# Moving a layer's output stores from SyncE's queue to ScalarE's, with one input pair and some weight preparation moved to later groups

## The chip, the cores and the metric

The kernel runs on one core of a Trainium2 chip. The metric is the device time of one execution in microseconds, from launch to end. A profiled execution also has a span, from the first to the last instruction of the core, and a granted clock of TensorE.

## The reference, cut to what matters

The input x has the shape (4, 16, 512, 512). Four residual layers follow each other, each with a group normalisation in front of a convolution. The change touches the first layer only, and in it the first of its two blocks:

```
x = x + L0(gn(x))            # 8 groups of 2 channels for each image
L0: y = block1(gn(x)); z = block2(y)
block(v): for every channel, its triplet of neighbouring channels is convolved with three
          reflected 5x5 kernels of dilation 1, 2 and 4, weighted by a, b, c, summed, then tanh
x = x + L1(gn(x))            # 3x3 convolution of quantised values
x = x + L2(gn(x))            # 17x17 box filter
x = x + L3(gn(x))            # convolution in the frequency domain
```

## The kernel before, in words

Function `layer0` holds the whole first layer. The work of a block is cut into units u: an image b, a pair of channels p (8 pairs for each image) and a half of the rows, so NU = 64 units for a block and 16 for an image. A unit has four groups g, and n = 4u + g counts groups: n = 0 to 255 is the first block, 256 to 511 the second. For a first-block group TensorE runs 27 offsets times 4 matmuls (L726) from a window tile `win[half]`, which holds the rows of neighbouring channels as two fp16 halves. ScalarE takes the result out of PSUM through tanh (`evict`, L804), VectorE splits it into a high and a low fp16 part in the tile `yt[u % 2]` (`halves`, L631 and L633), GpSimd mirrors the margins (L896), and the group's rows are stored to the DRAM tensor `ys` (`store_y`, L957). A group makes two such stores; it makes three where p is 0 or 7, that is in the first two and the last two units of an image, because the edge channels are written twice.

The windows are loaded two units ahead from the DRAM tensor `xs` (`load`, L939): two transfers for a group, four where p is 0. A load for unit u waits for the matmuls that read the same place of the window in unit u - 2. In the units with u % 16 == 2, and in unit 0, the four loads are put together behind the third group (`late`).

`xs` is made in the same stretch. For a pair i of input channels (32 in all, 8 for each image) there are four steps z = 0 to 3 in four consecutive groups, starting at `first_group(i)`: statistics on VectorE (`v0`, L457), their sums over partitions by two small matmuls (`p0`, L703 and `p1_`, L707), the root on ScalarE (`root_step`, L240, with an activation table load before and after it), the scaling and the split (`v2` L473, `hi` L795, `v3` L479), the margins (L851), and the store of the pair (`store_xs`, L912). Pairs 0 and 1 come before the first group, pair 2 has steps around groups 0 and 1, pair 3 starts at group 4, pair 4 at group 11, and then one every 7 groups. The input of pair i (`load_x`, L905) is loaded 4 and 6 groups after the start of pair i - 2.

The order on each engine is written out by hand. SyncE's queue issues, for each group n in turn: the store of a finished pair, the window loads of two units later, the stores of `ys` for group n (each waits for the margins of group n, semaphore `c_pad`), and the next quarter of input. ScalarE's order for a group is: root, evict, `hi`. An eviction of group n waits for VectorE's `halves` of group n - 3, and a group's matmuls wait for the eviction of group n - 4, because there are four PSUM banks and three tiles `c_t`. `halves` of the first group of a unit waits until all `ys` stores of unit u - 2 have landed (`c_yd`).

`channel_weights` (L548 to L577) and `scaled_weights` on VectorE make weights for later layers. The first follows a matmul (L783) behind group 8 and ends in a sum for which TensorE waits with a matmul (L786) behind group 11. The second comes in group 15, with a root on ScalarE.

Of the kernel before, what the change touches and what calls it, by code (L numbers as in the profile page):

```python
# [16 lines left out]
RW = 2 * PW  # L17
CP = 32 * RW
VP = 2 * CP
# [264 lines left out]
def layer0(K):  # L284
# [6 lines left out]
    NU = NB * 16  # L291
    NG = 8 * NB

    with ExitStack() as ctx:
# [62 lines left out]
        def place(u):  # L357
            blk, r = divmod(u, NU)
            b, q = divmod(r, 16)
            return blk, b, q // 2, q % 2  # L360

        def first_group(i):

            image, j = divmod(i - 3, 8)
            return 64 * image + 4 + 7 * j if i > 2 else -2

        steps = {first_group(i) + z: (i, z) for i in range(2, NG) for z in range(4) if first_group(i) + z >= 0}
        loads_x = {first_group(i - 2) + 4 + 2 * c: (i, c) for i in range(4, NG) for c in range(2)}
# [81 lines left out]
        with nc.Block() as block:  # L450

            @block.vector
            def _(v):
# [223 lines left out]
                for u in range(2 * NU):  # L677
                    blk, b, p, half = place(u)
                    for g in range(4):
                        if doubled(4 * u + g + 1):  # L680
                            copies(4 * u + g + 1)
                        i, s = stage_of(4 * u + g)
                        if i is not None:
                            (v0, v1, v2, v3)[s](i)
                        if (u, g) == (2, 0):
                            mark["v"] = ch.n
                        if (u, g) == (2, 1):
                            channel_weights()
                        if (u, g) == (3, 3):
                            scaled_weights()  # L690
                        if table_of(u) is not None and g % 2 == 0:
                            table(table_of(u), g // 2)
                        (total if blk else halves)(u, g)
                        if blk:
                            extremes(u, g)
                    if blk:
                        gather(u)

            @block.tensor
            def _(p):  # L700
                def p0(i):
                    p.wait_ge(a_v, mark["m", i])
                    p.matmul(ap[:, 0:1], ones[:, :], am[:, :, 0], start=True, stop=True).then_inc(a_p, 1)  # L703

                def p1_(i):
                    p.wait_ge(a_v, mark["d", i])
                    p.matmul(ap[:, 1:2], ones[:, :], d0, start=True, stop=True).then_inc(a_p, 1)  # L707

                def products(u, g):
                    blk, b, pr, half = place(u)  # L710
                    n = 4 * u + g
                    pg, buf, wu = pp[:, n % 4, :], win[half], wc2[pr % 2] if blk else wc[pr % 2][:, 0]
                    rows_in(p, u, g)
                    if (u, g) == (2, 0):
                        p.wait_ge(w_sw, 32)
                    if (u, g) == (NU, 0):
                        p.wait_ge(w_s2, 16 * 24)
                        p.wait_ge(w_wn, 12)
                    if n >= 4:
                        p.wait_ge(c_act, n - 3)  # L720

                    def four(weights, source, at, start=False, stop=False):
                        for j in range(4):
                            bk = 4 * g + j
                            var = 0 if (half, bk) == (0, 0) else (2 if (half, bk) == (1, 15) else 1)
                            t = p.matmul(pg[32 * j:32 * j + 32, :], weights[:, var], source[:, j, at:at + NW],  # L726
                                         start=start, stop=stop, tile_position=(0, 32 * j))
                        return t

                    rows4 = buf[:, 4 * g:4 * g + 4]  # L730
                    for di in (4, 0, 1, 7, 8):
                        for wl, xl in ((0, 0), (0, 1), (1, 0)):
                            four(wu[:, wl, :, di], rows4, xl * PW + PAD + DX[di], start=(di, wl, xl) == (4, 0, 0))
                    i, s = stage_of(n - 1)
                    if s == 0:
                        p0(i)
                    if s == 1:
                        p1_(i)
                    for di in (2, 3, 5, 6):
                        t = four(wu[:, 1, :, di], rows4, PAD + DX[di])  # L740
                    if not blk:
                        for di in (2, 3, 5, 6):
                            for xl in range(2):
                                t = four(wu[:, 0, :, di], rows4, xl * PW + PAD + DX[di], stop=(di, xl) == (6, 1))
                    if blk:
                        p.wait_ge(c_nh, n_copied(n))
                        p.wait_ge(c_nl, n_copied(n))
                        for e, di in enumerate((2, 3, 5, 6)):
                            four(wn2[pr % 2][:, :, e], near[n % 2], PAD + DX[di])
                        p.wait_ge(c_2a, n_copied(n))  # L750
                        p.wait_ge(c_2b, n_copied(n))
                        four(wn2[pr % 2][:, :, 4], twice[n % 2], PAD - 2)
                        t = four(wn2[pr % 2][:, :, 5], twice[n % 2], PAD - 1, stop=True)
                    t.then_inc(c_pe, 1)

                p0(0)
                p1_(0)
                p0(1)
                p1_(1)
                p.wait_ge(w_ld, 320)  # L760
                p.wait_ge(a_v, mark["we"])
                for d in range(3):
                    t = p.matmul(p1[0:96, 0:18], emb[:, d, :], we[:, :, d, :], start=d == 0, stop=d == 2)
                t.then_inc(w_p, 1)
                p.wait_ge(a_v, mark["sum"])
                p.matmul(p1[:, 32:34], ones[0:27, :], c2[0:27, 0:2], start=True, stop=True).then_inc(w_p, 1)
                p.wait_ge(w_sel, 16)
                p.wait_ge(a_v, mark["cch"])
                for var in range(3):
                    for col in range(32):  # L770
                        t = p.matmul(p3[:, var, col // 16, 18 * (col % 16):18 * (col % 16) + 18], sel[:, var, col, :],
                                     cch[:, :], start=True, stop=True)
                t.then_inc(w_p, 1)
                p0(2)
                p1_(2)
                p.wait_ge(a_v, mark["wc"])
                for u in range(2 * NU):
                    for g in range(4):
                        products(u, g)
                        if (u, g) == (2, 0):  # L780
                            p.wait_ge(w13_ld, 160)
                            p.wait_ge(a_v, mark["v"])
                            p.matmul(pq[:, 0:432], rep[:, :], w16[:, :, :].rearrange("p j n -> p (j n)"), start=True, stop=True).then_inc(w13_p, 1)  # L783
                        if (u, g) == (2, 3):
                            p.wait_ge(a_v, mark["g3"])
                            p.matmul(pq[:, 0:1], ones[:, :], c2b[:, 0:1], start=True, stop=True).then_inc(w13_p, 1)  # L786

            @block.scalar
            def _(s):
# [17 lines left out]
                def copies(n):  # L807
                    w = four_rows(s, n)
                    s.activation(twice[n % 2][64:128, :, PAD - 2:PAD - 1 + NW], w[0:64, :, PW + PAD + 1:PW + PAD + 2 + NW], ACT.Copy).then_inc(c_2b, 1)  # L809
                    s.activation(twice[n % 2][0:64, :, PAD - 2:PAD - 1 + NW], w[0:64, :, PW + PAD - 2:PW + PAD - 1 + NW], ACT.Copy).then_inc(c_2a, 1)  # L810

                for blk in range(2):
                    pre = f"L0_conv_blk{blk + 1}_"
                    for d, nm in enumerate("abc"):
# [16 lines left out]
                for u in range(2 * NU):  # L831
                    for g in range(4):
# [2 lines left out]
                            copies(4 * u + g + 1)  # L835
                        if st_ == 2:
                            root_step(s, a_v, mark["rt", i], a_rt, ve, sq)
                        if (u, g) == (3, 3):
                            root_step(s, a_v, mark["sv"], w13_rt, c2b[:, 1:2], c2b[:, 2:3])
                        evict(u, g)  # L840
                        if st_ == 2:
                            hi(i)

            @block.gpsimd
            def _(q):
# [53 lines left out]
            def _(e):  # L899
# [49 lines left out]
                    for m in range(2):  # L949
                        e.dma_start(xwin(u)[m::2], rows(x, u, m, NW, NH * NW)).then_inc(c_xd[u % 2], 16)  # L950

                def store_y(u, g):
                    blk, b, p, half = place(u)
                    e.wait_ge(c_pad, 8 * u + 2 * g + 2)
                    y = yt[u % 2][:, g].rearrange("p l w -> p (l w)")
                    for m, gp, slot in [(0, p, 1), (1, p + 1, 0)] + [(1, 0, 0)] * (p == 0) + [(0, 8, 1)] * (p == 7):
                        e.dma_start(dram(ys, pair(b, gp, slot, 16 * half) + g * 4 * RW, [[RW, 4], [VP, 16], [1, RW]]), y[m::2]).then_inc(c_yd[u % 2], 16)  # L957

                def store_x1(u, g):
                    e.wait_ge(c_lo, 4 * u + g + 1)  # L960
                    blk, b, p, half = place(u)
# [32 lines left out]
                for u in range(2 * NU):  # L994
                    blk, b, p, half = place(u)
                    late = u < NU and u % 16 == 2 or u == 0
                    for g in range(4):
# [14 lines left out]
                                load(u + 2, gg)  # L1012
                        if blk:
                            store_x1(u, g)
                        else:
                            store_y(u, g)
                        if g == 0 and NU + 2 <= u + 1 < 2 * NU:
                            load_res(u + 1)
                        if g == 0 and u in (NU - 4, NU - 3):
# [1056 lines left out]
```

## Time and profile before

| | |
|---|---|
| median of 3 runs | 5208.22 us (5204.88 to 5220.45) |
| profiled execution, its own time | 5213.77 us |
| its span | 5212.0 us |
| mean granted TensorE clock | 0.986 |
| TensorE matmul busy | 4885.1 us, 94% of the span |
| first block's groups, first matmul to last | 71.4 to 1669.8 us |

Times within the trace are microseconds from the start of the span. The busy share of TensorE is high, so what can be won or lost lies in the places where it waits, and in the half clock that follows some of these waits.

### The profile page before, as it was taken

Reading aid. Unit: us, or ns where it says so; the run is one execution under the profiler, and the core shown is the slowest. Engines: PE = TensorE matmul, PEld = TensorE weight load, DVE = VectorE, ACT = ScalarE, POOL = GpSimd, SP = SyncE. Lnnn points to the kernel's source line nnn. Section 1 sums busy time; section 2 is a strip of 40 time slices with the busy share of each in tenths; the row PEclk is TensorE's granted clock in tenths of the full one; section 3 lists DMA queues with packets and bytes.
Section 4 is the critical chain, followed back from the end, with each engine's and each line's share of the span. In section 5 each row is a group of like instructions: output and inputs, shape, how many; then the busy total and the mean of one; then the engine's idle time right before and its main releaser. Section 6 shows DMA issues by size and latency. Waiting matters only on the chain. (4 is left out here: it accounts for less than half of the span.)

```text
span 5212.0 us, 176617 instructions
## 1 busy us (share of the span) xinstructions
PE 4885.1 (94%) x76605; PEld 2764.2 (53%) x76605; DVE 3722.4 (71%) x6707; ACT 3385.1 (65%) x3511; POOL 1419.1 (27%) x1641
## 2 busy tenths in 40 slices
PE   4999999999999999999999979997777899999998
PEld 2444444444445566555456653444555566666665
DVE  5653453453433888888888868887999688888888
ACT  2231222222222788888888878885998689899897
POOL 0000001000001222222222200002777255555556
PEclk9999999999999999999999989999999999999999
DMA  8777777677666788778787869996887465655664
GB/s 248 240 256 232 232 251 240 229 254 240 221 225 182 233 221 228 234 222 243 231 233 238 221 210 325 323 323 243 309 308 269 115 152 149 153 149 153 153 149 120
DMA packets 355854, 1167.09 MB, mean 224 GB/s; under 512 B 58409, under 2 KB 59048, under 8 KB 285226
## 3 DMA queue, kind: packets, MB, share of 16 engines
q1 hardware_dynamic: 352920, 1153.41, 72.0%
q8 instruction: 606, 9.93, 0.8%
q10 hardware_dynamic: 2162, 2.39, 0.2%
q14 instruction: 166, 1.36, 0.1%
HBM read 683.58 MB, written 453.51 MB: 218 GB/s over the span
## 5 line engine op out<-in xcount | busy, mean ns | idle before, releaser
L726 PE MATMUL c_p<-c_w,wc 128*32 128x512 f16 x27648 | 1527.6, 382 | 25.3 <-DMA c_w<-xs 22.5
L804 ACT ACTIVATE c_t<-c_p,cbias,cscale 128x512 f32<-128x512 f32 x512 | 398.1, 778 | 1292.0 <-PE c_p L726 1292.0
L726 PEld LDWEIGHTS c_p<-c_w,wc 128*32 128x32 f16 x27648 | 737.6, 97 | 786.7 <-issue 34.7
L726 PE MATMUL c_p<-c_w,w 128*32 128x512 f16 x19456 | 1131.6, 379 | 7.0 <-issue 5.6
L726 PEld LDWEIGHTS c_p<-c_w,w 128*32 128x32 f16 x19456 | 641.7, 96 | 431.7 <-issue 12.8
L631 DVE TENSOR_SCALAR c_y<-c_t 128x512 f16<-128x512 f32 x256 | 109.6, 428 | 702.7 <-ACT c_t L804 576.6
L1801 PE MATMUL f_P<-f_qh,f_wt 64*64 64x512 f16 x4608 | 545.7, 378 | 1.8 <-DVE f_t L1697 1.8
L1801 PE MATMUL f_P<-f_hl,f_wt 64*64 64x512 f16 x4608 | 545.3, 379 | 0.0
L809 ACT ACTIVATE c<-c_w 64x2052 f16<-64x2052 f16 x256 | 492.5, 1924 | 12.3 <-DMA c_w<-ys 6.0
L810 ACT ACTIVATE c<-c_w 64x2052 f16<-64x2052 f16 x256 | 493.0, 1926 | 6.3
L1962 POOL TENSOR_TENSOR f_y<-f_y,f_x 128x512 f32<-128x512 f32 x256 | 331.1, 1293 | 448.1 <-DVE f_hl L1676 442.0
L896 POOL COPY c_y<-c_y 128x16 f16<-128x16 f16 x512 | 88.5, 203 | 1269.0 <-DVE c_y L633 1269.0
L1697 DVE SCALAR_TENSOR_TENSOR f_t<-f_P,f_kk,f_ci 128x256 f32<-128x256 f32 x1024 | 423.5, 476 | 11.9 <-PE f_P L1801 7.2
L1561 POOL TENSOR_TENSOR e_hl<-e_g,e_hl 128x2048 f16<-128x2048 f32 x63 | 257.3, 4083 | 608.0 <-ACT e_hl L1511 608.0
L1762 PE MATMUL f_qp<-f_hil,f_gT 128*128 128x260 f16 (+1 forms) x3120 | 393.4, 276 | 4.0 <-DVE f_qh L1681 4.0
L1801 PEld LDWEIGHTS f_P<-f_hl,f_wt 64*64 64x64 f16 x4608 | 232.9, 106 | 255.0 <-issue 77.7
L1190 PE MATMUL d_pp<-d_q,wq 128*128 128x512 f16 x1536 | 345.9, 381 | 16.9 <-DVE d_q L1087 16.9
L1968 POOL TENSOR_TENSOR f_t<-f_t 128x512 f32<-128x512 f32 (+1 forms) x260 | 334.1, 1285 | 71.8 <-DVE f_hl L1676 71.8
L1936 ACT ACTIVATE f_y<-f_P,f_kk,sv 128x256 f32<-128x256 f32 x512 | 261.3, 561 | 127.5 <-PE f_P L1801 121.2
L641 DVE TENSOR_TENSOR a_x<-c_t,a_x 128x512 f32<-128x512 f32 x256 | 192.7, 753 | 199.9 <-ACT c_t L804 174.5
L1762 PEld LDWEIGHTS f_qp<-f_hil,f_gT 128*128 128x128 f16 (+1 forms) x3120 | 295.2, 98 | 42.2 <-issue 4.9
L1681 DVE SCALAR_TENSOR_TENSOR f_qh<-f_qp,f_qh 128x520 f16<-128x520 f32 (+1 forms) x260 | 181.9, 700 | 179.9 <-ACT f_qh L1915 179.8
(274 smaller groups left out, 7789.2 us busy)
## 6 DMA issues: line engine op xcount, KB each, us to landing
c_w<-xs SPq DMA_DIRECT2D x576, 264.0 KB, 7.6
d_x<-x SPq DMA_DIRECT2D x128, 1024.0 KB, 7.7
x<-d_x SPq DMA_DIRECT2D x128, 1024.0 KB, 5.1
ys<-c_y SPq DMA_DIRECT2D x576, 132.0 KB
c_w<-ys SPq DMA_DIRECT2D x144, 528.0 KB
xs<-a_hl SPq DMA_DIRECT2D x70, 1056.0 KB, 11.4
a_x<-in_x SPq DMA_DIRECT2D x256, 256.0 KB, 5.7
a_x<-in_x SPq DMA_DIRECT2D x128, 512.0 KB, 4.9
```

Source lines behind the costliest of these rows:

```text
L726: t = p.matmul(pg[32 * j:32 * j + 32, :], weights[:, var], source[:, j, at:at + NW], start=start, stop=stop, tile_position=(0, 32 * j))
L804: s.activation(tt_[n % 3][:, :], pp[:, n % 4, :], ACT.Tanh, bias=cbias[:, blk:blk + 1], scale=cscale[:, blk:blk + 1]).then_inc(c_act, 1)
L809: s.activation(twice[n % 2][64:128, :, PAD - 2:PAD - 1 + NW], w[0:64, :, PW + PAD + 1:PW + PAD + 2 + NW], ACT.Copy).then_inc(c_2b, 1)
L810: s.activation(twice[n % 2][0:64, :, PAD - 2:PAD - 1 + NW], w[0:64, :, PW + PAD - 2:PW + PAD - 1 + NW], ACT.Copy).then_inc(c_2a, 1)
L1190: t = p.matmul(pp[:, 4 * (i % 2) + j, :], wq[:, wl, dx, :], qt[i % NQ][:, j, dx:dx + NW], start=(i < 2 and dx == 0 and wl == 0), stop=(i > ...
L1561: q.tensor_tensor(h[:, 1], gt[i % 2][:, :, :], h[:, 0], ALU.subtract).then_inc(e_lo, 1)
L1697: v.scalar_tensor_tensor(dst[0:n, z], src[:, 256 * z:256 * z + 256], k_[0:n, off + z:off + z + 1], cc_[0:n, j, z], op, ALU.mult).then_inc( ...
L1762: t = p.matmul(qp[0:n, a_, 0:260], T[:, xl, 1 - a_, kx, 0:n], hil[:, wl, 1 - a_, kx, :], start=z == 0, stop=z == 5)
L1801: t = p.matmul(P[64 * z:64 * z + 64, bank, :].rearrange("p (a i) -> p a i", a=2), w[k0:k0 + 64, wl, f, :], r[k0:k0 + 64, l, :, 0:256], sta ...
L1936: s.activation(y0[i % 3][0:n, z], P[0:n, 0, 256 * z:256 * z + 256], ACT.Identity, bias=k_[0:n, 6 + z:7 + z], scale=inv(i)).then_inc(f_y0, 1)
L1962: q.tensor_tensor(y0[i % 3][:, :, :], y0[i % 3][:, :, :], par(xin[i % NXF][:, :]), ALU.add).then_inc(f_ax, 1)
L1968: q.tensor_tensor(t1[i % 3][0:n], t1[i % 3][0:n], t2[i % 2][0:n], ALU.add).then_inc(f_aw, 1)
```

## The change

The stores of `ys` leave SyncE's queue. ScalarE issues those of group n - 1 in its turn of group n, behind the eviction of n and behind `hi` if there is one, so the first block's last group is stored in the first turn of the second block. Pair 3 starts at group 6 in place of 4, and the input of pair 5 is therefore loaded at groups 10 and 12 in place of 8 and 10. The first weight matmul moves from behind group 8 to behind group 14, `channel_weights` from group 9 to 15, the second weight matmul from behind 11 to behind 17, and `scaled_weights` from group 15 to 22. No instruction is added or left out.

```
-            return 64 * image + 4 + 7 * j if i > 2 else -2
+            return 64 * image + 4 + 7 * j + 2 * (i == 3) if i > 2 else -2
...
-                        if (u, g) == (2, 0):
+                        if (u, g) == (3, 2):
                             mark["v"] = ch.n
-                        if (u, g) == (2, 1):
+                        if (u, g) == (3, 3):
                             channel_weights()
-                        if (u, g) == (3, 3):
+                        if (u, g) == (5, 2):
                             scaled_weights()
...
-                        if (u, g) == (2, 0):
+                        if (u, g) == (3, 2):
                             p.wait_ge(w13_ld, 160)
...
-                        if (u, g) == (2, 3):
+                        if (u, g) == (4, 1):
                             p.wait_ge(a_v, mark["g3"])
...
+                def store_y(u, g):
+                    blk, b, p, half = place(u)
+                    s.wait_ge(c_pad, 8 * u + 2 * g + 2)
+                    y = yt[u % 2][:, g].rearrange("p l w -> p (l w)")
+                    for m, gp, slot in [(0, p, 1), (1, p + 1, 0)] + [(1, 0, 0)] * (p == 0) + [(0, 8, 1)] * (p == 7):
+                        s.dma_start(dram(ys, pair(b, gp, slot, 16 * half) + g * 4 * RW, [[RW, 4], [VP, 16], [1, RW]]), y[m::2]).then_inc(c_yd[u % 2], 16)
...
-                        if (u, g) == (3, 3):
+                        if (u, g) == (5, 2):
                             root_step(s, a_v, mark["sv"], w13_rt, c2b[:, 1:2], c2b[:, 2:3])
                         evict(u, g)
                         if st_ == 2:
                             hi(i)
+                        if 1 <= 4 * u + g <= 4 * NU:
+                            store_y(*divmod(4 * u + g - 1, 4))
...
                         if blk:
                             store_x1(u, g)
-                        else:
-                            store_y(u, g)
```

## Rows read from the trace of the kernel before

**Rows 1.** Waits of TensorE, then of SyncE's queue, over the first block's groups.

```profile
PE a_p L707 <- DVE f_t L465: 22.7, 3, 9.6
PE c_p L726 <- DMA c_w<-xs: 22.5, 7, 5.9
PE a_p L703 <- DVE a_mv L459: 6.1, 2, 4.1
PE a_p L786 <- DVE c2b L577: 3.9, 1, 3.9
...
SPq L957 <- POOL c_y L896: 44.9, 46, 5.3
```

**Rows 2.** ScalarE's timeline: evictions of groups 68, 80, 132, 144, 196, 208.

```profile
502.25 0.78 ACT L804 ACTIVATE c_t<-c_p,cbias,cscale 128x512 f32<-128x512 f32 x1 [5.06 <-PE c_p L726]
...
596.23 0.78 ACT L804 ACTIVATE c_t<-c_p,cbias,cscale 128x512 f32<-128x512 f32 x1 [13.64 <-PE c_p L726]
...
907.46 0.78 ACT L804 ACTIVATE c_t<-c_p,cbias,cscale 128x512 f32<-128x512 f32 x1 [5.06 <-PE c_p L726]
...
995.63 0.78 ACT L804 ACTIVATE c_t<-c_p,cbias,cscale 128x512 f32<-128x512 f32 x1 [13.14 <-PE c_p L726]
...
1304.93 0.78 ACT L804 ACTIVATE c_t<-c_p,cbias,cscale 128x512 f32<-128x512 f32 x1 [5.06 <-PE c_p L726]
...
1392.53 0.78 ACT L804 ACTIVATE c_t<-c_p,cbias,cscale 128x512 f32<-128x512 f32 x1 [11.47 <-PE c_p L726]
```

**Rows 3.** TensorE's timeline at the first image boundary.

```profile
522.87 0.59 PE L707 MATMUL a_p<-f_t,ones 128*128 128x1 f32 x2 [9.59 <-DVE f_t L465]
...
587.62 12.66 PE L726 MATMUL c_p<-c_w,wc 128*32 128x512 f16 x184 [5.86 <-DMA c_w<-xs]
```

**Rows 4.** VectorE's timeline there, and its waits over the block.

```profile
521.13 0.43 DVE L631 TENSOR_SCALAR c_y<-c_t 128x512 f16<-128x512 f32 x1 [17.60 <-DMA ys<-c_y]
...
DVE c_y L631 <- DMA ys<-c_y: 124.2, 13, 17.6
```

**Rows 5.** SyncE queue's timeline there: issues, with start and length.

```profile
506.40 2.60 SPq L957 DMA_DIRECT2D ys<-c_y  x3
...
533.74 3.44 SPq L957 DMA_DIRECT2D ys<-c_y  x3
537.28 1.76 SPq L939 DMA_DIRECT2D c_w<-xs  x2
539.09 3.29 SPq L957 DMA_DIRECT2D ys<-c_y  x3
```

**Rows 6.** DMA view of 510 to 550 us: 40 slices of 1 us.

```profile
DMA  4883223973222893226952269532398222298322
GB/s 133 264 302 129 101 97 123 294 247 150 101 87 99 272 344 115 101 95 188 342 194 96 95 177 308 222 126 87 127 291 275 106 112 111 95 285 315 141 88 101
```

**Rows 7.** DMA view of 71 to 1670 us: issues.

```profile
c_w<-xs SPq DMA_DIRECT2D x566, 264.0 KB, 8.1
ys<-c_y SPq DMA_DIRECT2D x567, 132.0 KB
xs<-a_hl SPq DMA_DIRECT2D x67, 1056.0 KB, 11.5
a_x<-in_x SPq DMA_DIRECT2D x232, 256.0 KB, 5.6
```

**Rows 8.** Timeline at the start: TensorE's waits, ScalarE's eviction of group 5.

```profile
111.70 0.59 PE L703 MATMUL a_p<-a_mv,ones 128*128 128x1 f32 x2 [4.07 <-DVE a_mv L459]
...
130.59 6.02 PE L726 MATMUL c_p<-c_w,wc 128*32 128x512 f16 x108 [2.18 <-DMA c_w<-xs]
...
116.37 0.78 ACT L804 ACTIVATE c_t<-c_p,cbias,cscale 128x512 f32<-128x512 f32 x1 [11.16 <-PE c_p L726]
```

**Rows 9.** SyncE queue's stores: in a quiet stretch (600 to 841), and at the start.

```profile
L957 SPq DMA_DIRECT2D ys<-c_y x84: 542/568/2338, 600.0 to 841.0; - x84
...
100.81 13.53 SPq L957 DMA_DIRECT2D ys<-c_y  x6
```

More of the change, by code:

```diff
@@ L950, in load_res @@
                         e.dma_start(xwin(u)[m::2], rows(x, u, m, NW, NH * NW)).then_inc(c_xd[u % 2], 16)
[L952 to L957, printed above, removed]
                 def store_x1(u, g):
```

## The prediction

> **What bounds the kernel now.** I read the waits first. Over the first block's groups TensorE waits for four things: the statistics matmuls for VectorE (22.7 and 6.1 us), the window loads (22.5 us), and once for the weight sum (3.9 us) [rows 1]. That is 55 us in which nothing else stands in its way; the rest of the block's 1598 us is matmuls. So this change can win only in these places and in the half clock behind them, and it can lose wherever it makes a new one.
>
> Then I read where the waits lie. A quiet group takes 5.84 us: 0.78 of eviction and 5.06 of idle time on ScalarE [rows 2]. Two evictions twelve groups apart should be 70.0 us apart, and up to 2.4 more where four of the groups carry statistics matmuls (0.59 us each [rows 3]). At the three image boundaries it is 93.98, 88.17 and 87.60 us [rows 2]. The excess is 21.6, 15.8 and 15.2 us, together 52.6.
>
> Third, who makes it. In the first of them TensorE waits 9.59 us in a statistics matmul and 5.86 us for a window [rows 3]; the other 6 us are slower matmuls behind these waits and small gaps. VectorE is late for the statistics because it stands for 17.60 us in front of tile `c_y`, until the stores of the unit before the last have landed; over the block it stands so for 124.2 us [rows 4]. The last of those stores was issued at 506.40 to 509.00 and the tile came free at 521.13 [rows 4, 5]. So a store lands about 12 us after SyncE is rid of it: it isn't issue alone that is late, there is a queue of work behind it.
>
> Fourth, what the queue waits for. SyncE is solid here: 3.44 us for three stores, 1.76 for two loads, 5.35 us from one group's stores to the next (533.74 to 539.09) [rows 5]. One reads this easily as an issuing engine at its limit. But a store takes 0.568 us to issue in a quiet stretch [rows 9], and here 1.1. The slices say why: between short bursts of 264 to 344 GB/s the DMA engines are busy for two to three tenths, at 87 to 127 GB/s [rows 6]. The stores run on about a quarter of the 16 engines, and that quarter is full. The bursts are the loads, which use all.
>
> From this I price the full quarter: a store moves 132 KB at about 100 GB/s, 1.35 us. Three of them leave (5.35 - 4.05) / 2 = 0.65 us for a load of 264 KB, so 2.6 us for a store of `xs` (1056 KB) and 0.63 for 256 KB of input. Over the block that makes 567 x 1.35 + 566 x 0.65 + 67 x 2.6 + 232 x 0.63 = 765 + 368 + 174 + 146 = 1453 us [rows 7], 91% of 1598. In a quiet group it is 2 x 1.35 + 2 x 0.65 + (8 x 0.63 + 2 x 2.6) / 7 = 5.5 us of 5.84. In the eight groups before an image boundary (three stores, four loads) it is 4.05 + 2.6 + 1.5 = 8.15, in the eight behind it 6.85. The overload is 8 x 2.3 + 8 x 1.0 = 26 us; buffers take some of it, and 15 to 22 are left as the excess seen.
>
> **The change part by part.**
>
> *The stores' queue.* SyncE loses 567 issues and their `c_pad` waits (44.9 us [rows 1]); its loads go out as soon as the window is free. ScalarE gets these issues. In quiet groups two cost 2 x 0.57 = 1.1 us of 5.06 idle: nothing, covered by that idle time. In the turn with root and `hi` there is less room, but an eviction may be three groups late (17.5 us) before TensorE waits for its bank, so again nothing; without that cover it would be 1.1 us in 30 turns, 33 us. The wait on `c_pad` is for the group before, 5.84 us old, so it is met. Where VectorE is held up it isn't, and behind it stand the next eviction, then VectorE's next `halves`, then the matmuls four groups on.
>
> The 52.6 us are another matter. The quarter has the same 26 us too much at each boundary, whoever issues. Only what the buffers can take differs. Before, loads and stores were one line, so both were late together. Now they are two lines. The loads have eight groups of lead and need it less; the stores stand alone in theirs, and their lateness becomes ScalarE's, because a full ring holds the issuing engine (that is what 1.1 us for an issue of 0.57 shows). Each side of it has a bound. Below: the loads give way, the stores land in time and all 52.6 us go. Above: the trace shows three stores at 13.53 / 2 = 6.8 us at the start, where all engines are full [rows 9]. With 0.78 of eviction that is 7.6 us a group, 1.7 over 5.84, in 48 boundary groups 82 us. I take +5 us for each boundary, +15: nearest to the row of the full quarter, 3.44 + 0.78 = 4.2 us [rows 5], which fits in 5.84 but leaves little when a root and `hi` come in the same turn.
>
> The Trainium skill (DMA: Bandwidth & Descriptors, "Issuing engines are not separate DMA queues") says that issuing from several engines saves only the issuing time, as all share the same 16 engines. By it the boundaries keep their 52.6 us, a term of 0 here in place of my +15.
>
> *Pair 3 two groups later.* TensorE waits 4.07 us in group 5 for the statistics of pair 3, and eviction 5 comes 0.78 + 11.16 = 11.94 us after eviction 4, 6.1 too many [rows 8]. Two groups are 11.7 us, more than the 4.07 that its input was late: -6. The 2.18 us for the window of group 8 [rows 8] should go as well, since the loads of unit 2 no longer queue behind six stores that took 13.53 us [rows 9]: -2. Against that the pair's store comes two groups later, and the loads of unit 4 wait for it; they are issued at group 11 for group 16, 29 us of lead against 11.5 of landing for the store and 8.1 for a load [rows 7]: nothing, and 10 us if it fails. Stores of both queues fill the start, where the engines are full anyway: +2. Sum -6, from -8 to +4.
>
> *The weights.* The same 50-odd instructions and two matmuls in the same distance (6 groups later, between statistics steps in the same way): TensorE's 3.9 us wait for the sum [rows 1] goes along. ScalarE's turn 16 now holds a store that waits for VectorE to finish them. Before, VectorE began them in the turn of group 9 and TensorE waited 3.9 us for their end behind group 11, so they end some 3 x 5.84 + 3.9 = 21 us after their group begins; the eviction of group 17 is due at 17.5 and comes 4 us late or a little more, within 17.5. Term 0, from -2 to +4.
>
> *The end of the block.* ScalarE stores groups 254 and 255 in turns that also hold the second block's copies: -0, +5, taken as 0.
>
> Sum: +15 - 6 + 0 = +9 us on 5213.77 (span 5212.0 and 1.8 around it), which is 5.5 above the median: 5208.22 + 9, about **5217 us**.
>
> **The rivals.** (1) *The boundary waits go.* If what is full is SyncE's line and not the quarter of the engines, the stores are issued right behind the next eviction (four groups before that of 502.25 [rows 2], so at about 480 in place of 506), VectorE's 17.6 us vanish, and TensorE loses none: -52.6 - 8 = -61, 5147 us; with half the effect 5178. For it: SyncE has no gap there [rows 5]. Against: 1.1 us for an issue that needs 0.57, and slices at two tenths [rows 6]. The Trainium skill (Perfetto Trace Analysis, "DMA Optimizations") recommends it: if descriptor generation is the bottleneck, spread the DMAs over issuing engines, and loads and stores over two. That would be this case. Chance 0.27.
>
> (2) *ScalarE is held by its stores.* Slower: if an issue at the boundaries takes over (5.84 - 0.78) / 3 = 1.69 us, ScalarE falls behind for good, evictions come late, and TensorE waits for banks. At 2.25 us it is +82; with the start's gain and some groups below that, +20 to +80, say 5250 us. It also decides if loads and stores share the engines piece by piece, since a load's pieces are larger. For it: the start's row [rows 9]. Against: the full quarter itself needs only 1.35 us for a store. Chance 0.25.
>
> (3) *It does nothing.* The wait keeps its size and only its name changes, 5208 - 6 = 5202 us. Chance 0.10.
>
> **How the numbers follow.** The forecast has 0.38; its own range is 5195 to 5240. 0.3% is 15.6 us, about what a measurement of this kernel can tell. Below 5192.6 lies most of rival 1 and a little of the forecast: 0.29. Above 5223.8 lies rival 2 and a quarter of the forecast: 0.34. The rest, 0.37, is within. The range leaves out the far parts of rivals 1 and 2: 5160 to 5265.
>
> **What would show it.** Right: in 440 to 600 us the DMA slices keep their stretches of two to three tenths; VectorE waits less for `ys` but for ScalarE instead; issues on ScalarE take about 1.1 us at the boundaries; evictions twelve groups apart there still are 88 to 100 us apart; groups 4 and 5 are 5.8 to 6.3 apart. Wrong: boundaries at 72 us (rival 1), or evictions late in quiet stretches too, with TensorE waiting for ScalarE (rival 2). The forecast fails if the engines serve the two queues unevenly: then either the loads or the stores take the whole overload, and eight groups of lead or three groups of banks decide it.

## The result, and the profile after

The changed kernel takes 5251.76 us (median of 4 runs, 5241.35 to 5257.96), the kernel before 5207.48 in the same comparison: a ratio of 1.0075, 95% interval 1.0061 to 1.009. It is slower by 0.75%, 32 to 47 us by the interval and 44 by the medians, where 5217 was forecast; 5251.76 lies in the range, on the side of the second rival (ScalarE is held by its stores, 5250). The profiled span is 5248.3 us against 5212.0, 36.3 more, and the mean granted clock 0.983 against 0.986.

Where the time went is read from one kind of row, the evictions on ScalarE's timeline (L804), taken at the same group in both traces. Groups are counted by the evictions themselves, 512 in each trace; two that follow each other without a gap stand in one merged row of a timeline. The column on the right is how late the changed kernel is.

| eviction of group | before, us | after, us | after is late by |
|---|---|---|---|
| 4 | 104.43 | 103.43 | -1.0 |
| 22 | 229.26 | 238.51 | 9.3 |
| 50 | 396.18 | 405.80 | 9.6 |
| 80 (first boundary passed) | 596.23 | 605.41 | 9.2 |
| 144 (second) | 995.63 | 1006.53 | 10.9 |
| 208 (third) | 1392.53 | 1406.32 | 13.8 |
| 250 | 1640.62 | 1654.15 | 13.5 |
| 256 | 1675.63 | 1716.61 | 41.0 |
| 270 | 1757.19 | 1789.90 | 32.7 |

So the start (groups 4 to 22) costs 10.3 us, the stretches with the three boundaries 4 us together, and the end of the block 27.5, of which 8.3 come back in the second block's first groups. Of the 36.3 us between the spans, 32.7 are there at group 270.

The waits of the changed kernel, from 71 to 1740 us, which takes in the first block and the second's first groups: engine, tile and line, what it waited for, then the sum in us, times, the longest.

```profile
ACT c_t L804 <- PE c_p L726: 906.4, 214, 14.5
DVE c_y L631 <- ACT c_t L804: 729.2, 162, 31.4
ACT c_t L804 <- issue: 224.0, 28, 31.8
...
PE a_p L703 <- DVE a_mv L459: 43.0, 5, 11.8
PE c_p L726 <- DVE c_n L662: 20.9, 1, 20.9
...
PE c_p L726 <- ACT c_t L804: 14.9, 4, 6.5
...
PE a_p L786 <- DVE c2b L577: 5.7, 1, 5.7
PE c_p L726 <- DMA c_w<-xs: 3.7, 1, 3.7
```

TensorE's waits add up to 88 us where they were 55 in the block [rows 1], or 59 up to 1740 us. The window loads are no longer late (3.7 us for 22.5), and VectorE waits no more for stores of `ys` (124.2 us [rows 4]): it waits for ScalarE. ScalarE in turn has 224 us of idle time ahead of evictions that nothing released but its own issuing. A reader who looks at TensorE's releasers alone would blame VectorE (64 us); VectorE waits for an eviction, and the eviction for an issue.

ScalarE's timeline shows what it issues: at the start, before the first image boundary, and at the end of the block.

```profile
103.43 9.71 ACTq L817 DMA_DIRECT2D ys<-c_y  x3
113.25 0.78 ACT L804 ACTIVATE c_t<-c_p,cbias,cscale 128x512 f32<-128x512 f32 x1 [9.04 <-issue]
113.27 10.43 ACTq L817 DMA_DIRECT2D ys<-c_y  x3
...
453.36 10.43 ACTq L817 DMA_DIRECT2D ys<-c_y  x3
...
469.63 15.49 ACTq L817 DMA_DIRECT2D ys<-c_y  x3
485.23 0.78 ACT L804 ACTIVATE c_t<-c_p,cbias,cscale 128x512 f32<-128x512 f32 x1 [14.85 <-issue]
485.26 14.56 ACTq L817 DMA_DIRECT2D ys<-c_y  x3
...
1667.38 32.46 ACTq L817 DMA_DIRECT2D ys<-c_y  x3
1699.95 0.78 ACT L804 ACTIVATE c_t<-c_p,cbias,cscale 128x512 f32<-128x512 f32 x1 [31.80 <-issue]
```

Three stores hold ScalarE for 10, 15 and once 32 us, where the group leaves 5.06. Behind the last of them stand the eviction at 1699.95, 28 us after its matmuls were done, VectorE's work on it, and TensorE, which waits 20.9 us for its next input `c_n` until 1708.29. The grouped issues of line 817 give the usual figure beside it (shortest, median and longest in ns; 200 to 440 us, then 445 to 545 us):

```profile
L817 ACTq DMA_DIRECT2D ys<-c_y x80: 515/527/5599, 206.7 to 438.0; - x80
...
L817 ACTq DMA_DIRECT2D ys<-c_y x39: 515/1282/9437, 447.5 to 539.9; - x39
```

The queue of SyncE, in the same two places:

```profile
472.13 8.58 SPq L948 DMA_DIRECT2D c_w<-xs  x12
...
482.87 28.30 SPq L948 DMA_DIRECT2D c_w<-xs  x10
...
1659.98 16.65 SPq L944 DMA_DIRECT2D c_w<-ys  x16
...
1683.32 5.77 SPq L944 DMA_DIRECT2D c_w<-ys  x8
1718.12 1.14 SPq L965 DMA_DIRECT2D x<-a_x  x2
```

Its loads go in bursts now; [rows 5] has two loads between two lots of stores. From 1689.09 to 1718.12 it issues nothing, and ScalarE is held until 1699.84 all the same. So it isn't an issue of SyncE that ScalarE waits for there.

The DMA view of 510 to 550 us, as in [rows 6]. There are now twelve slices in a row at 91 to 99 GB/s, at two tenths:

```profile
DMA  2794223972327853222222222222329842228932
GB/s 97 215 376 150 112 96 126 294 275 108 137 87 190 289 218 123 93 91 99 95 97 97 97 97 97 95 99 95 116 95 272 243 190 114 84 101 240 361 138 115
```

### The profile page after: what moved, and what is told of

It reads as the page before. It is cut to its first block and busy times, and to the rows that moved or that the text cites. A ratio compares the mean times of both kernels' runs of the same rounds, so it can differ in the third digit from the quotient of the medians.

```text
span 5248.3 us, 176617 instructions
## 1 busy us (share of the span) xinstructions
PE 4885.4 (93%) x76605; PEld 2851.3 (54%) x76605; DVE 3721.2 (71%) x6707; ACT 3384.2 (64%) x3511; POOL 1413.9 (27%) x1641
## 5 line engine op out<-in xcount | busy, mean ns | idle before, releaser
L804 ACT ACTIVATE c_t<-c_p,cbias,cscale 128x512 f32<-128x512 f32 x512 | 397.8, 777 | 1351.9 <-PE c_p L726 1107.2
L726 PEld LDWEIGHTS c_p<-c_w,w 128*32 128x32 f16 x19456 | 700.2, 96 | 368.7 <-issue 11.4
L726 PE MATMUL c_p<-c_n,w 128*32 128x512 f16 x4096 | 298.2, 380 | 23.0 <-DVE c_n L662 22.1
## 6 DMA issues: line engine op xcount, KB each, us to landing
xs<-a_hl SPq DMA_DIRECT2D x70, 1056.0 KB, 10.8
```

Of the source, the lines that this page charges most:

```text
L804: s.activation(tt_[n % 3][:, :], pp[:, n % 4, :], ACT.Tanh, bias=cbias[:, blk:blk + 1], scale=cscale[:, blk:blk + 1]).then_inc(c_act, 1)
```

## The experiments

The expectations name theories by letters. A is the second rival's mechanism: the stores run on a quarter of the engines, that quarter is full, and the engine that issues them is held. The others are rivals to it: SyncE's issuing is the limit (D), the two queues share something that makes the descriptors (E), loads and stores share an engine piece by piece, so that the size of a load's pieces decides (F), or only the engines' total time counts and not who is served first (G). Lines below are those of the changed kernel where nothing else is said. Each ratio is to the kernel before in the same comparison.

**1. The stores alone.** The changed kernel with pair 3 and both weight steps at their old places.

```
-            return 64 * image + 4 + 7 * j + 2 * (i == 3) if i > 2 else -2
+            return 64 * image + 4 + 7 * j if i > 2 else -2
...
-                        if (u, g) == (3, 2):
+                        if (u, g) == (2, 0):
...
```

> Only the stores' queue moves to ScalarE; pair 3 and the weights stay where they were. Theory A (the stores on ScalarE's queue carry the whole loss, because a load burst of SyncE holds the engines that the stores need): 5245 to 5265 us, +40 to +57 over before, with issues of three stores of 10 to 32 us on ScalarE at the start, at the image boundaries and at the end of the block. Rival B (the moved steps carry part of the loss): under 5235 us.

5252.59 us (5244.29 to 5256.62), ratio 1.0074 (1.005 to 1.0097). The whole loss is the stores'. The wait for the weight sum is 16.2 us here and 5.7 in the changed kernel, so the later weights seem to ease what the stores do at the start, though not in a total that can be measured. The rival that expected under 5235 us is out.

**2. The steps alone.** The kernel before with pair 3 and the weights moved, and the stores left with SyncE.

```
-            return 64 * image + 4 + 7 * j if i > 2 else -2
+            return 64 * image + 4 + 7 * j + 2 * (i == 3) if i > 2 else -2
...
-                        if (u, g) == (2, 0):
+                        if (u, g) == (3, 2):
...
```

> Only pair 3 and the weights move; the stores stay on SyncE's queue in their old form. After the run with the stores alone gave the whole loss, theory A: these steps are worth -2 to -8 us, as the 4.07 us wait in group 5 and the 2.18 us wait for the window of group 8 go and the wait for the weight sum moves along. Rival B: they cost 5 us or more, through the later store of pair 3 or a collision of the weights with the next pair.

5213.73 us (5208.26 to 5222.69, 12 runs), ratio 1.0012 (1.0004 to 1.0021): no gain. TensorE's timeline at the start says why:

```profile
127.64 5.97 PE L726 MATMUL c_p<-c_w,wc 128*32 128x512 f16 x60 [6.46 <-DMA c_w<-xs]
...
197.66 0.59 PE L786 MATMUL a_p<-c2b,ones 128*128 128x1 f32 x2 [5.42 <-DVE c2b L577]
```

The wait of 4.07 us in group 5 is gone, and the window of group 8 is 6.46 us late in place of 2.18 [rows 8]. The wait was returned one step further on. (The changed kernel doesn't have this wait: with the stores off SyncE's queue, TensorE ends group 11 at 147.61 us where it was 155.14.)

**3. The loads held back.** SyncE waits for the margins of each group in the place where it used to store, and issues nothing there.

```
+                        else:
+                            e.wait_ge(c_pad, 8 * u + 2 * g + 2)
```

> The changed kernel, but SyncE waits for the margins of group n where its stores of group n were, without storing. Theory A with the burst as its cause (SyncE, rid of these waits, sends the second block's first loads in one burst of 16): the stall of 32 us in the last groups of the block goes down to under 10, total 5215 to 5230 us. Theory C (any load in flight is enough, the order of issue does not matter): within 5 us of the changed kernel, 5247 to 5257 us.

5243.73 us (5237.82 to 5249.33), ratio 1.0055 (1.0035 to 1.0075). By the medians the bursts account for about 8 us, which the intervals don't settle, and the 5215 to 5230 expected was missed. At the end of the block three stores still take 21.70 us, where under 10 was expected. So bursts lengthen one stall; they aren't alone what makes the stores slow.

**4. The stores on all engines, issued by SyncE.** In the kernel before, the two plain stores of a group become four, one for each row. On the DRAM side their outer dimension is the 16 row blocks (`[VP, 16]`) and not the 4 rows (`[RW, 4]`).

```
-                    for m, gp, slot in [(0, p, 1), (1, p + 1, 0)] + [(1, 0, 0)] * (p == 0) + [(0, 8, 1)] * (p == 7):
-                        e.dma_start(dram(ys, pair(b, gp, slot, 16 * half) + g * 4 * RW, [[RW, 4], [VP, 16], [1, RW]]), y[m::2]).then_inc(c_yd[u % 2], 16)
+                    for j in range(4):
+                        e.dma_start(dram(ys, pair(b, p, 1, 16 * half) + (g * 4 + j) * RW, [[VP, 16], [31 * CP, 2], [1, RW]]),
+                                     y[32 * j:32 * j + 32]).then_inc(c_yd[u % 2], 16)
+                    for m, gp, slot in [(1, 0, 0)] * (p == 0) + [(0, 8, 1)] * (p == 7):
+                        ...
```

> The kernel before, with the two plain stores of a group written as four, each of 32 partitions with the 16 row blocks outermost on the DRAM side; the extra edge store stays. Same bytes and pieces. Theory A (a store in the old form runs on a quarter of the 16 engines, that quarter is full): the stores spread over all engines, the slices of two to three tenths vanish, boundaries fall from 88 to 94 us to 72 to 78 for twelve groups, total 5140 to 5165 us. Rival D (SyncE's issuing is the limit): 2 more issues of 0.57 us a group on a queue that is solid at the boundaries, total 5215 to 5240 us.

5235.53 us (5220.06 to 5241.72), ratio 1.0036 (1.002 to 1.0053): slower, where theory A expected 5140 to 5165. D had it right. SyncE's queue at the first boundary, and the DMA slices of 510 to 550 us:

```profile
507.18 2.49 SPq L957 DMA_DIRECT2D ys<-c_y  x4
509.71 0.57 SPq L960 DMA_DIRECT2D ys<-c_y  x1
510.39 2.65 SPq L939 DMA_DIRECT2D c_w<-xs  x4
513.08 2.51 SPq L957 DMA_DIRECT2D ys<-c_y  x4
```

```profile
DMA  9989975689697318999868863797469754378952
```

The stretches of two tenths are gone, most slices are at six to nine, so the work of the quarter is now spread. But the queue is still solid, now with each issue at its shortest, 0.6 us. Nine of them and their gaps take 5.9 us (507.18 to 513.08), and a group has 5.84. Here "solid" means what it seemed to mean in [rows 5], and there did not.

**5. The same stores issued by ScalarE.** The changed kernel with the four stores of experiment 4 in place of its two.

> The changed kernel with the stores spread in the same way, issued by ScalarE. Theory A (ScalarE is held by pieces in full engines): with 2 pieces for each engine and store nothing holds it, 5130 to 5165 us. Rival E (ScalarE's issue waits until SyncE's issue is through, as if one generator served both): twice the issues, twice the waits: 5250 to 5300 us.

5193.03 us (5186.34 to 5206.06), ratio 0.9965 (0.9952 to 0.9978), 59 us under the changed kernel though it issues almost twice as many stores. The row of ScalarE's queue from 71 to 1740 us (packets, MB, share of 16 engines), first of the changed kernel, then of this one:

```profile
q10 hardware_dynamic: 39168, 77.87, 12.7%
```

```profile
q10 hardware_dynamic: 53504, 77.92, 15.4%
```

39168 is 576 x 68: 64 pieces and 4 more for each store. 53504 is 1024 x 48 + 64 x 68: 32 pieces and 16 more for each new store. If the additional packets are one completion for each engine that a store uses, the old form uses 4 and the new one 16. The Trainium skill (DMA: Bandwidth & Descriptors, "Why a DMA increments its semaphore by 16 and not by 1") says just this: the number of engines is the largest one up to 16 that divides the slowest dimension of both sides, and each posts one completion. The old store has a slowest dimension of 4 on its DRAM side and of 64 on the other; the packets agree.

At the boundary the stores' issues now have a median of 617 ns where it was 1282:

```profile
L817 ACTq DMA_DIRECT2D ys<-c_y x69: 537/617/4092, 443.0 to 544.5; - x69
```

This speaks against E: almost twice the stores, and no issue above 4.1 us in this row. The expected 5130 to 5165 was missed all the same. What is left is, it seems, ScalarE's own time. Four or five issues of 0.6 us leave 2.1 to 2.7 of 5.06 us, which a turn with root and `hi` exceeds, and ScalarE's own issues stand ahead of 58 evictions with 374.7 us of idle time, 6.5 us each. Experiment 7 tries this.

**6. Only the third store spread.** In the changed kernel, the third store that the first and last pair of an image have is cut in four, each with 16 as the outer dimension; the plain stores stay.

```
+                    for m, gp, slot in [(1, 0, 0)] * (p == 0) + [(0, 8, 1)] * (p == 7):
+                        for j in range(4):
+                            s.dma_start(dram(ys, pair(b, gp, slot, 16 * half) + (g * 4 + j) * RW, [[VP, 16], [1, RW]]),
+                                        y[32 * j + m:32 * j + 32:2]).then_inc(c_yd[u % 2], 16)
```

> The changed kernel, with only the third store of edge groups written as four of 16 partitions; the two plain stores keep their old form. Theory A (a quarter of the engines is full at the image boundaries because of the third store): the boundary's load on that quarter falls from 8.15 and 6.85 us a group to about 7.1 and 5.8, the long issues of 10 to 15 us become fewer, and the total is 5210 to 5235 us. Rival D (the number of issues on ScalarE counts): six issues in place of three at the boundaries, 5255 to 5280 us.

5227.29 us (5221.08 to 5231.77), ratio 1.003 (1.0019 to 1.004). Taking a third of the load off the quarter in these groups, with more to issue, is worth 24 us. It bears out A: less load on the quarter, less loss.

**7. Spread, and the issuing shared.** SyncE issues rows 0 and 1 in its old place, ScalarE rows 2 and 3 and the third store.

```
+                    for j in (2, 3):
+                        s.dma_start(dram(ys, pair(b, p, 1, 16 * half) + (g * 4 + j) * RW, [[VP, 16], [31 * CP, 2], [1, RW]]),
+                                     y[32 * j:32 * j + 32]).then_inc(c_yd[u % 2], 16)
...
+                    e.wait_ge(c_pad, 8 * u + 2 * g + 2)
+                    y = yt[u % 2][:, g].rearrange("p l w -> p (l w)")
+                    for j in (0, 1):
+                        e.dma_start(...)
```

> The spread stores of the fifth run, but rows 0 and 1 of a group are issued by SyncE in the old place and rows 2 and 3 and the edge store by ScalarE. If what is left at 5193 us is ScalarE's time (5 issues of 0.62 us, beside root and hi) and in the fourth run SyncE's (6 to 9 issues a group), sharing helps both: 5150 to 5180 us. If SyncE's wait for the margins in front of its loads is what costs, it is 5190 to 5210 us.

5164.99 us (5164.37 to 5172.88), ratio 0.9918 (0.9904 to 0.9931). It beats both kernels, and experiment 5 by 28 us, so the time of issuing did count there.

**8. Small pieces, by another address pattern.** The loads of the first block with a dimension of its own for the rows.

```
-                                        dram(src, at + h8 * (8 * VP - RW), [[CP, 16], [RW, 2], [1, 4 * RW]])).then_inc(c_ld[half][g], 16)
+                                        dram(src, at + h8 * (8 * VP - RW), [[CP, 16], [RW, 2], [RW, 4], [1, RW]])).then_inc(c_ld[half][g], 16)
```

> The changed kernel, with the first block's window loads written as rows of 2112 bytes in place of runs of 8448 (same bytes, four times the pieces). Theory F (an engine that has work from both queues takes one piece from each in turn, so four times larger load pieces starve the stores): the pieces are now equal, three stores at a boundary take 4 to 7 us in place of 10 to 15 on ScalarE, and the total falls to 5215 to 5235 us. Rival G (the engines' time is what is short, whoever is served first): no change or slower, 5245 to 5270 us. If the run of four rows is joined again on its way to the engines, nothing changes and the trace still shows pieces of 8448 bytes.

5250.2 us (5243.58 to 5259.16), ratio 1.0079 (1.0063 to 1.0095). It says nothing: the trace has no more packets than before, so adjacent rows were joined again and the edit changed no piece.

**9. Half pieces in the first block.** Each of its loads becomes two, of two rows each, with pieces of 4224 bytes in place of 8448; the stores are as in the changed kernel.

```
+                            for r in (0, 2):
+                                e.dma_start(win[half][gp % 2 + 2 * h8:128:4, 4 * g + r:4 * g + r + 2].rearrange("p k w -> p (k w)"),
+                                            dram(src, at + h8 * (8 * VP - RW) + r * RW, [[CP, 16], [RW, 2], [1, 2 * RW]])).then_inc(c_ld[half][g], 16)
```

> The changed kernel, with every window load of the first block cut into two transfers of two rows, so that its pieces are 4224 bytes in place of 8448 (the earlier try was joined to 8448 again). Same bytes; SyncE issues 4 or 8 loads a group in place of 2 or 4. Theory F (an engine takes one piece of each queue in turn): at the boundaries 48 store pieces took 14.6 to 15.5 us, about 0.3 us each, as if each waited for one load piece of 0.2 to 0.4 us; with pieces half as large the longest issues of three stores there are 8 to 11 us and the total is 5222 to 5242 us. Rival G (only the engines' total time counts): the longest stay at 13 to 16 us, total 5247 to 5265 us.

5242.56 us (5239.74 to 5245.22), ratio 1.0049 (1.0034 to 1.0064) to 5218.74. ScalarE's timeline before the first boundary, the turns of groups 60 and 61:

```profile
469.37 10.31 ACTq L817 DMA_DIRECT2D ys<-c_y  x3
...
479.81 7.85 ACTq L817 DMA_DIRECT2D ys<-c_y  x3
```

15.49 and 14.56 us have become 10.31 and 7.85, as F has it. But later turns take longer in return: the stores of turns 58 to 68 take 78.1 us together, where they took 80.4. The total moves by less than the two comparisons can settle.

**10. Half pieces at the end of the block.** Only the second block's loads are cut in two: pieces of 8448 bytes in place of 16896.

```
+                                for r in (0, 4):
+                                    e.dma_start(win[half][first + gp % 2:first + 2 * count:2, 4 * g + r:4 * g + r + 4].rearrange("p k w -> p (k w)"),
+                                                dram(src, at + off + r * RW, [[CP, count], [1, 4 * RW]])).then_inc(c_ld[half][g], 16)
```

> The changed kernel, with the second block's window loads (whose first ones stand beside the last stores of the first block) cut in two, pieces of 8448 bytes in place of 16896. Theory F: the issue of three stores that took 32.5 us at the end of the block takes 16 to 22, and the total falls by 8 to 15 us, to 5237 to 5244 us. Rival G: it stays at 29 to 34 us and the total within 4 us of the changed kernel.

5249.91 us (5245.66 to 5253.85), ratio 1.0063 (1.0048 to 1.0078). ScalarE's timeline in place of the one issue of 32.46 us:

```profile
1665.73 11.20 ACTq L817 DMA_DIRECT2D ys<-c_y  x3
...
1677.06 14.16 ACTq L817 DMA_DIRECT2D ys<-c_y  x3
...
1691.35 12.01 ACTq L817 DMA_DIRECT2D ys<-c_y  x3
```

The longest hold is less than half as long, in the direction of F. But the same three turns sum to 37.4 us where it was 40.6 (32.46, 3.68 and 4.41), so next to nothing is won, and the 5237 to 5244 of F was missed. It looks as if the hold ends when the loads in front of the quarter are through, not after a number of stores. Nor is the piece the only thing that changed: SyncE now issues twice as many loads, and 32 of them take 25.58 us where 16 took 16.65, so the loads come more slowly too.

**11. The version of experiment 7 with the old steps.** Pair 3 and the weights back at their places.

> The shared, spread stores of the seventh run, with pair 3 and the weights where they were before the change. The run with the moved steps alone was 0.12% slower than before, since the wait in group 5 came back as a wait for the window of unit 2. If the steps are no help with spread stores either: 5155 to 5165 us. If they are, because the loads now come in time: 5168 to 5178 us.

5160.54 us (5157.48 to 5165.2), ratio 0.9895 (0.9878 to 0.9911). The interval overlaps that of experiment 7, so moving the steps later brings nothing here either. ScalarE before the first boundary:

```profile
484.46 0.78 ACT L804 ACTIVATE c_t<-c_p,cbias,cscale 128x512 f32<-128x512 f32 x1 [5.06 <-PE c_p L726]
484.46 1.19 ACTq L817 DMA_DIRECT2D ys<-c_y  x2
485.68 0.56 ACTq L820 DMA_DIRECT2D ys<-c_y  x1
490.29 0.78 ACT L804 ACTIVATE c_t<-c_p,cbias,cscale 128x512 f32<-128x512 f32 x1 [5.06 <-PE c_p L726]
```

Each issue takes its shortest time, each eviction waits 5.06 us for TensorE as in a quiet group, and the groups are 5.83 us apart. TensorE's waits in the block's groups are 3.4 us for windows, 5.5 and 2.8 for VectorE, and 11.8 in small gaps of issue.

## Why the prediction was right or wrong

**What bounds the kernel: right.** The reading that a quarter of the engines is full, and not SyncE, holds: the packets (experiment 5), the gain from taking load off it (5, 6, 7), and the slices that fill up (4). One part was too strong. Once the stores are spread, SyncE's issuing is the next limit, and a close one (4). The first rival, that the boundary waits simply go, came out wrong for the reason given: 1.1 us for an issue of 0.57, and slices at two tenths.

**The stores' queue at the boundaries: +15 forecast, 4 measured.** The direction and the mechanism were right, the size too high. The lateness did move from VectorE's wait for stores to ScalarE's issues, as "their lateness becomes ScalarE's" says, and it came earlier: ScalarE is late from turn 58 on, and TensorE loses time in groups 66 and 69, where it did in 70 and 80. The length of an issue, named as about 1.1 us, has a median of 1.28 but is very uneven; three of them took up to 15.49.

**The start: -6 forecast, +10.3 measured.** The first half of the forecast, -8 for pair 3 and the window, came about in the changed kernel: the last matmul of group 11 ends 7.5 us earlier than before, 1.0 of it because a weight matmul now comes later. (With the stores left on SyncE it doesn't, by experiment 2.) The step that failed is "Stores of both queues fill the start, where the engines are full anyway: +2". That the engines are full is no cover when the engine that is held is the one that evicts. ScalarE's turns 4 to 6 hold it for 9.71, 10.43 and 11.98 us, its eviction of group 9 comes 14.75 us after its matmuls, VectorE's statistics of pair 4 stand behind these evictions, and TensorE waits for them in group 12. Group 12 ends 20.90 us after group 11; before it was 14.44, with the wait for the weight sum in it.

```profile
162.69 0.58 PE L703 MATMUL a_p<-a_mv,ones 128*128 128x1 f32 x2 [11.84 <-DVE a_mv L459]
...
205.02 0.59 PE L786 MATMUL a_p<-c2b,ones 128*128 128x1 f32 x2 [5.68 <-DVE c2b L577]
```

So the held stores cost some 15 us at the start (20.90 in place of a quiet 5.84), where +2 was forecast. The row for it was in hand: six stores in 13.53 us [rows 9], which was used as an upper bound for the boundaries and not applied to the start itself, where it was read.

**The end of the block: 0 forecast, with +5 as its bound; +27.5 measured, 8.3 of them given back.** This is the largest miss, and the bound was wrong as well. The step is "ScalarE stores groups 254 and 255 in turns that also hold the second block's copies: -0, +5". It looked at ScalarE's work and not at what SyncE does there. SyncE, no longer held to a group's pace by its waits for `c_pad`, sent 16 of the second block's loads in one go at 1659.98 (before, eight went out between two lots of stores, 5.56 us at 1666.02), and the three stores of 1667.38 took 32.46 us among them. The forecast counted the waits that SyncE loses (44.9 us [rows 1]) as nothing but a gain for the loads.

**The weights: 0 forecast, about 0 measured.** What their sum cost in group 12, 14.44 us for 5.84, it costs in group 18 now, 14.27. The wait is 5.68 us for 3.93, and the eviction of group 17 comes 8.6 us late, not 4. The totals of experiments 1, 2 and 11 agree.

The terms measured, 10.3 + 4 + 19.2, come to 33.5 where +9 was forecast. So what took place is the second rival, and 5251.76 lies in the range because the range took it in. That its price, 5250, was so near is luck: it was priced by up to 82 us in 48 groups at the boundaries, which gave 4, and the loss came at the start and at the end of the block. Its second condition, "if loads and stores share the engines piece by piece, since a load's pieces are larger", is what experiments 9 and 10 agree with for the length of one hold. For the total they bear out little: 9 and 2 us by the medians. The sums of several turns hardly moved, so the total seems to follow the work that the quarter has before it.

**What stays open.** How an engine chooses between the two queues is seen only through these lengths. How much of the loss at the start is due to the loads that SyncE issues in it (sixteen for the windows from 116.36 us on), no run tells; with half the piece the evictions of groups 6 and 7 were 20.63 us apart, where it was 12.11 (experiment 9). The number of engines of a store and the piece size of the loads were not varied against each other, so the pieces' own share in the slow stores is open. At the end of the block there is one more candidate: two of every four loads of the second block have an outer dimension of 8 (L944). If they use 8 engines, as a store with 4 uses 4, and the stores' engines are among them, the stores stand behind more load pieces there; no run tries it.

## What to carry to other kernels

Before moving transfers to another queue, look at how many engines each of them uses: here an issue that took longer than its shortest time, beside DMA slices at two tenths, meant that a few engines were full, and the queue that seemed solid was not the first limit. ScalarE, issuing stores to full engines, was held for up to 32.46 us, and everything behind it in its order was late; so first spread the transfer (here with outer dimensions of 16 and 32 in its two address patterns, in place of 4 and 64), then share the issues among the queues (1.05% faster here, where moving alone was 0.75% slower). And a wait that is taken from a queue was also its pace: ask what the queue will send in one burst without it.

## What the runs showed of the hardware

- Three stores of 132 KB on four engines held the issuing ScalarE for 32.46 us, while SyncE's queue issued nothing in the last 10.8 us of it. In that time the engines still had work, by the windows of 6 us (the last three columns: granted clock, DMA share, GB/s):

```profile
1690.00:1696.00 6.00, 0.00 (x0) 0.00 (x0) 0.00 (x0) 0.00 (x0) 0.00 (x0) 0.59 0.67 181
1696.00:1702.00 6.00, 0.00 (x0) 0.00 (x0) 1.21 (x3) 0.78 (x1) 0.03 (x1) 0.50 0.29 108
```

- The longest hold went with the size of the other queue's pieces: three stores took up to 32.46 us beside loads with pieces of 16896 bytes and 11.20 to 14.16 us beside 8448 (both at the block's end), and 15.49 beside 8448 and 10.31 beside 4224 (both before the first boundary). The sum over several turns hardly changed (experiments 9 and 10). The Trainium skill (DMA: Bandwidth & Descriptors, "Queues, rings and completion order") says that an engine goes round the queues with work for it, a whole packet from each; the longest holds agree in direction, the sums don't show it.
- Rows that are adjacent in memory were joined into one piece though the address pattern held them apart (experiment 8).
- The Trainium skill (DMA: Bandwidth & Descriptors, "Issuing engines are not separate DMA queues") says that issuing from several engines saves only the time of the issuing. With a quarter of the engines full, moving the stores didn't give even that: 5251.76 us for 5207.48. For spread stores the time of issuing did count: 5235.53 us from SyncE, 5193.03 from ScalarE, 5164.99 from both.
